# Two-layer graph network on one core: the order of squares, weights and stores between the layers, of the loads in the second layer, and of its last groups

## The chip, the core and the metric

The kernel runs on one core of one Trainium2 chip. The metric is the device time of one execution in microseconds (us), the median of three runs. A core has engines with a program each: PE (TensorE, matrix products; PEld is its loading of weights), DVE (VectorE), ACT (ScalarE), POOL (GpSimd) and SP (SyncE, which here only issues transfers). They meet at semaphores alone. DMA engines move the data between HBM and the on-chip memory; a transfer is issued by SP, by ACT or, for the indexed ones, by POOL.

## The reference

12,500 nodes with 16 features and 412,500 edges (200,000 random pairs both ways and one loop per node), sorted by the node `dst`.

```python
edge_index = jnp.stack([src, dst])
h = relu(layernorm(x));  x = x + L0(h, edge_index, edge_attr_16, ...)
h = relu(layernorm(x));  x = x + L1(h, edge_attr_8, ..., edge_index)

# L0: messages by a small network on the edge, summed, then normalized over the nodes
hid = relu(edge_attr @ W1 + b1); w = (hid @ W2 + b2).reshape(-1, 16, 16)
aggr = segment_sum(einsum('ei,eio->eo', x[src], w), dst)
out = aggr + x @ root + bias
out = relu((out - mean) / sqrt(var + 1e-5) * gamma + beta)      # over all nodes

# L1: a product of node and edge features, summed by node
m = silu(einsum('ei,ej,ijh->eh', x[dst], edge_attr, W_msg_tp) / sqrt(128)) @ W_msg_lin / 4
agg = segment_sum(m, src)
u = silu(einsum('ni,nh,ihk->nk', x, agg, W_upd_tp) / 16) @ W_upd_lin / 4;  return x + u
```

## The kernel before, in words

The program has five stages one after the other, with a barrier of all engines after each: `setup`, `layer0`, `between`, `layer1`, `finish`. The edges are cut into G = 404 groups of 1024 (T = 8 tiles of 128). The node arrays `k.agg`, `k.x`, `k.h` hold 128 nodes by 98 blocks (B = 98) of 16 features.

**between** (L1164). DVE, ACT and PE normalize the sums of layer 0 over the nodes: DVE subtracts the mean from `k.agg` in two halves (49 blocks each, L1249) and raises `bn_centred` after each; ACT squares each half into `sq` (L1307, `bn_squared`); DVE sums the squares (L1255); PE adds over the partitions (L1347); then come the root, the scaling, the new x, and the layer norm, again with squares by ACT (L1318), until DVE writes `k.h` in two halves (L1281), with `h1_ready` after each. Ahead of its squares ACT stands waiting for eight small loads of the message weights (`bd_in`) and copies them into another order (L1302, `bd_turned`); after its root it does the same for the update weights (L1311, `bdu_turned`). Then `NodeLinear` (`lin`, L640) computes Q = h @ W_msg_tp for all nodes: per chunk c of T = 8 blocks PE transposes h (`turn`, L660), ACT copies the transpose (L686), PE multiplies it by the weights in pieces of 4 blocks (L672). Q is kept as three bf16 parts: ACT or DVE makes the first (L1334, L1291), DVE the rest (L1296), ACT the second (L1324, `q_mid`), POOL the third (L1199, `q_lo`), 25 pieces in all. SP stores 8 blocks (two pieces) at a time to `q_rows` in HBM (L1222), 13 stores for the QB = 100 blocks.

**layer1** (L1354). Every engine walks over the groups with a body of its own; buffers are double (s = g % 2), and a ring of four holds what is scattered.
- SP, `load(g)` (L1421): waits until the group before last has used all buffers (`mult1`, `hotT_ready`, `same_ready`, `gathered`), reads the window of the group from `win_i` into a register, and issues four loads: `q_win` (the 128 rows of Q around the group's nodes), `ea` (the edges' 8 features), `dst_row` (the group's 1024 indices, broadcast to 128 partitions, L1417), `src_row` (512 indices, broadcast, L1439). For group 0 alone `dst_row` goes first. After group 3 SP loads `k.xp`; after the last group it stores `k.h` and loads it in another layout.
- DVE, `body(g)`: `unit(g,0)` (product of the gathered Q and `ea`, L1501), `residue(g-1)`, sum (L1510), `one_hot(g+1)` (L1483, from `dst_row`), `rows_to(g-2)` (L1557, the rows of the scatter), `unit(g,1)`, `low(g-1)`, `half_low(g-1)`, sum, `place(g-1)` (L1544), `columns(g-1)` (L1534), `same_source(g+1)` (L1490, from `src_row`).
- ACT, `body(g)`: silu and the high parts, `squares(g)` (L1643), `mid(g)`, `total_out(g-1)` and `rows_out(g-1)` (L1630, L1635), `columns(g)` (L1649).
- PE, `body(g)`: `gather(g)` (L1682, 24 products), `sum_wide(g-2)` (L1708, 32 products), `sum_rows(g-1)` (L1695, 12 products): 68 products a group.
- POOL: four indexed transfers per group which add `total` to the tables `sums` in HBM (L1745).

After the loop stand the last steps in order. DVE: `residue(G-1)`, `low`, `half_low`, `place`, `columns` of G-1, then `rows_to(G-2)`, `rows_to(G-1)`, the wait for all wide sums and the addition to `acc` (L1597). PE: `sum_rows(G-1)`, `sum_wide(G-2)`, `sum_wide(G-1)`, then 14 transposes of `acc` (L1733), which ACT copies (L1669) and SP stores (L1460, L1463). `sum_rows(g)` waits for `total_ready` of the group before. `place(g)` waits for the wide sum of g-2.

## Time and profile before

| what | value |
|---|---|
| time before, median of 3 runs | 7299.28 us (7299.2 to 7299.56) |
| the profiled execution, its span | 8221.3 us |
| PE, DVE, POOL, ACT busy | 89%, 81%, 69%, 54% of the span |
| layer 0, from the start's end to | about 4985 us |
| between | about 4985.6 to 5055.1 us |
| layer 1 | 5055.1 to about 8137 us |
| finish | to 8221.3 us |

The profiled execution has no time of its own beside its span, 8221.3 us; it is 922 us longer than the median of the runs without the profiler. Stretches are given in us from the span's start. An engine's busy time is the sum over which one of its instructions was running; the clock is the one granted to TensorE, 1.0 being 2.4 GHz and 0.5 being 1.2 GHz. Idle time before an instruction is put down to the one that released it.

### The profile page before, as it was taken

How to read it: one execution, taken by the hardware profiler on the slowest of the kernel's cores; microseconds unless marked ns; L12 is line 12 of the kernel's file. 1: busy time of each engine (PE TensorE's matmuls, PEld its weight loads, DVE VectorE, ACT ScalarE, POOL GpSimd, SP SyncE). 2: the span in 40 equal slices, each digit the busy share in tenths (PEclk: the TensorE clock that was granted, in tenths of full speed). 3: DMA queues.
4: the chain of work that ended last, by engine and by line, in shares of the span. 5: the costliest groups of instructions: out<-in, count | busy, mean ns of one | idle time of the engine just before them, and what ended most of it. 6: DMA issues, size and time to landing. Idle time of an engine off the chain costs nothing. (4 is left out here: it accounts for less than half of the span.)

```text
span 8221.3 us, 191064 instructions
## 1 busy us (share of the span) xinstructions
PE 7349.2 (89%) x52997; PEld 6446.6 (78%) x52997; DVE 6691.0 (81%) x17449; ACT 4457.4 (54%) x8279; POOL 5696.0 (69%) x4866
## 2 busy tenths in 40 slices
PE   7888888888888888888888886999999999999998
PEld 5667676666676666666676765999999999999996
DVE  6777777777777777777777777999999999999997
ACT  3333333333333333333333335888888878778884
POOL 6666666666666666666666664888888888888886
PEclk8999999999999999999999998999999999999999
DMA  2000000000000000000000014444444455554443
GB/s 60 18 17 17 17 17 17 17 17 17 17 17 17 17 18 17 17 17 18 17 17 17 17 23 101 73 75 74 74 75 74 74 73 74 72 74 75 73 75 64
DMA packets 713464, 341.73 MB, mean 42 GB/s; under 512 B 422115, under 2 KB 656599, under 8 KB 713427
## 3 DMA queue, kind: packets, MB, share of 16 engines
q1 hardware_dynamic: 379313, 272.94, 13.1%
q0 software_dynamic: 332928, 64.86, 12.9%
q10 hardware_dynamic: 1186, 3.51, 0.1%
q8 instruction: 15, 0.25, 0.0%
q14 instruction: 22, 0.18, 0.0%
HBM read 307.85 MB, written 32.96 MB: 41 GB/s over the span
## 5 line engine op out<-in xcount | busy, mean ns | idle before, releaser
L802 POOL DMA_INDIRECT xg<-gather_rows,idx x3132 | 3041.9, 971 | 1882.4 <-issue 1848.5
L919 PE MATMUL ps_w<-W2s,hT 128*128 128x256 f32 x12928 | 3240.2, 408 | 37.1 <-issue 36.6
L919 PEld LDWEIGHTS ps_w<-W2s,hT 128*128 128x128 f32 x12928 | 2678.5, 207 | 581.6 <-issue 97.0
L1745 POOL DMA_INDIRECT sums<-total,row x1616 | 2551.0, 1579 | 529.1 <-issue 474.4
L1708 PE MATMUL ps_wide<-hot_col,placed 128*128 128x392 f32 x12928 | 2434.7, 345 | 4.8 <-DVE placed L1544 2.1
L1708 PEld LDWEIGHTS ps_wide<-hot_col,placed 128*128 128x128 f32 x12928 | 2313.6, 196 | 12.2 <-issue 6.9
L841 ACT ACTIVATE hT<-ps_h,b1c 128x512 f32<-128x512 f32 x1616 | 1022.8, 680 | 2302.1 <-PE ps_h L905 2090.8
L1002 DVE TENSOR_TENSOR prod<-ps_w,xg 128x512 f32<-128x512 f32 x1616 | 1098.1, 690 | 969.7 <-remote 599.7
L1544 DVE SCALAR_TENSOR_TENSOR placed<-ps_r,src_r,halves 128x512 fp32r<-128x512 f32 x1616 | 1097.5, 741 | 0.1
L1643 ACT ACTIVATE square<-iota_col,minus_col 128x784 bf16<-128x784 int16 x1212 | 1061.3, 938 | 66.6 <-issue 58.0
L1009 DVE TENSOR_REDUCE msg<-prod 128x32 f32<-128x512 f32 x1616 | 1058.9, 676 | 0.0
L1649 ACT ACTIVATE hot_col<-square,ones 128x2352 fp32r<-128x2352 bf16 x404 | 910.4, 2253 | 0.0
L933 PE MATMUL ps_a<-parts,hot 128*128 128x48 bf16 x6464 | 347.5, 184 | 549.8 <-issue 534.0
L1033 DVE TENSOR_SCALAR hot<-iota,rel_t 128x256 bf16<-128x256 bf16 x3232 | 729.1, 303 | 116.0 <-DVE ea_res L982 73.0
L933 PEld LDWEIGHTS ps_a<-parts,hot 128*128 128x128 bf16 x6464 | 249.8, 96 | 580.4 <-issue 566.4
L905 PE MATMUL ps_h<-eT,W1p 96*128 96x512 bf16 x1616 | 526.5, 401 | 147.5 <-issue 137.8
L1682 PE MATMUL ps_q<-q_win,hotT 128*128 128x128 bf16 x9696 | 609.6, 219 | 18.9 <-DVE hotT L1483 18.9
L1501 DVE TENSOR_TENSOR prod<-ps_q,e 128x512 f32<-128x512 f32 x808 | 552.3, 684 | 42.6 <-issue 40.4
L1682 PEld LDWEIGHTS ps_q<-q_win,hotT 128*128 128x128 bf16 x9696 | 548.1, 98 | 20.0 <-DVE hotT L1483 20.0
L1510 DVE TENSOR_REDUCE pre<-prod 128x64 f32<-128x512 f32 x808 | 548.3, 679 | 0.1
L851 ACT ACTIVATE parts<-msg_res 128x128 bf16<-128x128 f32 x404 | 124.9, 309 | 552.9 <-DVE msg_res L1021 322.9
L835 ACT ACTIVATE eT<-ps_e 96x1024 bf16<-96x1024 bf16 x404 | 409.1, 1013 | 1.9 <-PE ps_e L895 1.9
(229 smaller groups left out, 5425.0 us busy)
## 6 DMA issues: line engine op xcount, KB each, us to landing
dst_row<-dst_rows SPq DMA_DIRECT2D x404, 256.0 KB
src_row<-src_rows SPq DMA_DIRECT2D x404, 128.0 KB
xg<-gather_rows,idx POOLq DMA_INDIRECT x3132
q_win<-q_rows SPq DMA_DIRECT2D x404, 96.0 KB
ea<-in_edge_attr SPq DMA_DIRECT2D x404, 64.0 KB
sums<-total,row POOLq DMA_INDIRECT x1616
e<-in_edge_attr SPq DMA_DIRECT2D x404, 32.0 KB
q_rows<-Q SPq DMA_DIRECT2D x12, 768.0 KB, 5.4
```

Source lines behind the costliest of these rows:

```text
L802: pool.indirect_dma_start(xg[r][:, t, :], None, k.rows, bass.IndirectOffsetOnAxis(ap=idx[r][:, t:t + 1], axis=0)).then_inc(xg_in[r][t], 16)
L841: a.activation(hT[s][:, j, :], ps_h[j][:, :], ACT.Relu, bias=k.b1[:, j:j + 1]).then_inc(q["relued"], 1)
L919: last = pe.matmul(to, hT[half][:, j, col:col + P], k.W2[:, j, :], start=(j == 0), stop=(j == 1 and not with_b2))
L1002: v.tensor_tensor(prod[u % 2][:, :, :, :], ps_w[u][:, :, :, :], xg[r][:, 2 * u:2 * u + 2, 0:D].unsqueeze(2).broadcast_to([P, 2, D, D]), AL ...
L1009: v.tensor_reduce(msg[s][:, 2 * u:2 * u + 2, :], prod[u % 2][:, :, :, :], X, ALU.add).then_inc(q["reduced0"], 1)
L1033: last = v.tensor_scalar(hot[s][:, t, :], k.iota[:, :], k.rel[:, bass.ds(g, 1), t:t + 1].rearrange("p g t -> p (g t)"), None, ALU.is_equal)
L1544: last = v.scalar_tensor_tensor(placed[s][:, w, :, :, :].rearrange("p r f a -> p r (f a)"), ps_r[:, :, :], src_r[:, bass.ds(g, 1), w], hal ...
L1643: last = a.activation(square[:, n, :], iota_col[:, :], ACT.Square, bias=minus_col[:, bass.ds(g, 1), WIDE - ACT_TILES + n])
L1649: a.activation(hot_col[s][:, WIDE - ACT_TILES:, :, :].rearrange("p w a b -> p (w a b)"), square[:, :, :].rearrange("p w b -> p (w b)"), AC ...
L1682: last = pe.matmul(ps_q[u][:, w, :, :].rearrange("p h j -> p (h j)"), hotT[s][:, t * P:(t + 1) * P], q_win[s][:, part * P:(part + 1) * P], ...
L1708: last = pe.matmul(ps_wide[:, 2 * r + a, 0:S.LC], placed[s][:, w, r * HR:(r + 1) * HR, :, part].rearrange("p r f -> p (r f)"), hot_col[s][ ...
L1745: pool.indirect_dma_start(k.sums[t], bass.IndirectOffsetOnAxis(ap=row[r][:, t:t + 1], axis=0), total[r][:, t, :], None, compute_op=ALU.add ...
```

## The change

Between the layers, ACT squares the halves before it waits for and copies the message weights; the products of h start when the first half of h is there, and the transpose of the chunk that reaches over the middle (c = 6) waits for the second; the first store of 8 blocks becomes two of 4. In layer 1, `load(g)` no longer waits for all four buffers at its head: `dst_row` goes first behind the wait for `hotT_ready`, the window register and `q_win` behind `gathered`, `ea` behind `mult1`, `src_row` behind `same_ready`. Behind the loop, DVE does `rows_to(G-2)` right after `residue(G-1)`, and PE `sum_wide(G-2)` before `sum_rows(G-1)`.

```diff
     def tensor(self, pe, ident, second_half=None):
         def turn(c):
+            if second_half is not None and (c + 1) * T > self.S.B // 2 >= c * T:
+                pe.wait_ge(second_half, 2)
             need(pe, self.copied, c - 1)
...
+    stores = [0, 4, *range(T, S.QB, T), S.QB]
...
-        for b0 in range(0, S.QB, T):
-            b1 = min(b0 + T, S.QB)
+        for b0, b1 in zip(stores, stores[1:]):
             sp.wait_ge(n["q_lo"], b1 // 4)
...
-        sp.wait_ge(n["q_stored"], 16 * S.NC)
+        sp.wait_ge(n["q_stored"], 16 * (len(stores) - 1))
...
+        for i, (b0, b1) in enumerate(HALVES):
+            a.wait_ge(n["bn_centred"], i + 1)
+            a.activation(sq[:, b0:b1, :], k.agg[:, b0:b1, :], ACT.Square).then_inc(n["bn_squared"], 1)
         a.wait_ge(n["bd_in"], 16 * T)
         a.activation(bd_msg[:, :, :].rearrange("p b (h j) -> p b h j", j=J),
                      bd_jh[:, :, :].rearrange("p b (j h) -> p b h j", j=J),
                      ACT.Copy).then_inc(n["bd_turned"], 1)
-        for i, (b0, b1) in enumerate(HALVES):
-            a.wait_ge(n["bn_centred"], i + 1)
-            a.activation(sq[:, b0:b1, :], k.agg[:, b0:b1, :], ACT.Square).then_inc(n["bn_squared"], 1)
...
-        pe.wait_ge(n["h1_ready"], 2)
-        lin.tensor(pe, k.ident[:, :])
+        pe.wait_ge(n["h1_ready"], 1)
+        lin.tensor(pe, k.ident[:, :], second_half=n["h1_ready"])
...
-                    need(sp, q["mult1"], (g - 1) * 2)
                     need(sp, q["hotT_ready"], g - 1)
-                    need(sp, q["same_ready"], g - 1)
+                    rows_of_dst(g, s)
                     need(sp, q["gathered"], (g - 1) * 2)
-                    first = isinstance(g, int) and g == 0
-                    if first:
-                        rows_of_dst(g, s)
                     at = sp.value_load(k.win_i[0:1, bass.ds(g, 1)], min_val=0, max_val=P * (S.QB - 1))
                     sp.dma_start(q_win[s][:, :], k.q_rows[bass.ds(at, P), :]
                                  ).then_inc(in_sems["win_in"][s], 16)
+                    need(sp, q["mult1"], (g - 1) * 2)
                     sp.dma_start(ea[s][:, :, :].rearrange("p t f -> p (t f)"),
...
-                    if not first:
-                        rows_of_dst(g, s)
+                    need(sp, q["same_ready"], g - 1)
                     sp.dma_start(src_row[s][:, 0:TP, :].rearrange("p t f -> p (t f)"),
...
                 residue(G - 1, 1)
+                rows_to(G - 2, 0)
                 low(G - 1, 1)
...
                 columns(G - 1, 1)
-                rows_to(G - 2, 0)
                 rows_to(G - 1, 1)
...
+                sum_wide(G - 2, 0)
                 sum_rows(G - 1, 1)
-                sum_wide(G - 2, 0)
                 sum_wide(G - 1, 1)
```

## Rows read from the trace of the kernel before

**Rows 1.** Busy time by stretch: layer 0. From-to, length, PE, PEld, DVE, ACT, POOL busy, clock, DMA, GB/s.
```profile
200.00:5000.00 4800.00, 4070.98 (x24518) 3322.83 (x24516) 3495.35 (x9684) 1876.42 (x3931) 2957.03 (x3049) 0.92 0.10 18
```

**Rows 2.** The same view, three stretches of layer 1.
```profile
5200.00:6570.00 1370.00, 1370.00 (x12408) 1339.22 (x12407) 1337.07 (x3282) 1108.13 (x1825) 1147.52 (x730) 1.00 0.49 74
6570.00:7360.00 790.00, 786.17 (x7058) 763.20 (x7055) 761.71 (x1871) 627.17 (x1037) 663.43 (x416) 1.00 0.56 73
7360.00:8080.00 720.00, 720.00 (x6526) 703.85 (x6525) 704.42 (x1728) 582.77 (x961) 602.93 (x385) 1.00 0.48 74
```

**Rows 3.** Groups by line, DVE, 6570 to 7360: busy us, mean ns, idle before.
```profile
L1483 DVE TENSOR_SCALAR hotT<-dst_row,node_id 128x1024 bf16<-128x1024 int16 x104 | 53.7, 516 | 19.7 <-DMA dst_row<-dst_rows 17.5 <-issue 1.1
```

**Rows 4.** Timeline of one ordinary group of layer 1: start, length, engine, line.
```profile
6506.33 0.68 DVE L1501 TENSOR_TENSOR prod<-ps_q,e 128x512 f32<-128x512 f32 x1
...
6508.90 0.33 SPq L1417 DMA_DIRECT2D dst_row<-dst_rows  x1
...
6510.96 0.74 DVE L1490 TENSOR_SCALAR same<-src_row,src_t 128x128 bf16<-128x128 int16 x4
...
6512.94 0.48 DVE L1483 TENSOR_SCALAR hotT<-dst_row,node_id 128x1024 bf16<-128x1024 int16 x1
```

**Rows 5.** Timeline, a group in the second stretch of rows 2.
```profile
7011.26 1.91 POOL L1745 DMA_INDIRECT sums<-total,row  x1 [0.30 <-issue]
7011.66 1.01 DVE L1490 TENSOR_SCALAR same<-src_row,src_t 128x128 bf16<-128x128 int16 x4
```

**Rows 6.** Timeline of the stage between the layers.
```profile
4991.50 1.95 ACT L1302 ACTIVATE bd_msg<-bd_jh 128x1024 f32<-128x1024 f32 x1 [11.02 <-DMA bd_jh<-in_L_gnn_W_msg_tp]
...
4993.36 1.59 ACT L1307 ACTIVATE bn_sq<-aggn 128x784 f32<-128x784 f32 x2
...
4994.23 2.84 DVE L1255 TENSOR_REDUCE bn_s<-bn_sq 128x16 f32<-128x784 f32 x2 [1.54 <-ACT bn_sq L1307]
...
5002.49 3.75 ACT L1311 ACTIVATE dst_t<-rel_t 128x2048 f32<-128x2048 f32 x1 [3.87 <-DMA rel_t<-in_L_gnn_W_upd_tp]
...
5007.81 1.74 ACT L1318 ACTIVATE bn_sq<-hn 128x784 f32<-128x784 f32 x2 [1.57 <-DVE hn L1270]
...
5012.08 1.86 DVE L1281 SCALAR_TENSOR_TENSOR hn<-hn,ln_sd 128x784 f32<-128x784 f32 x2
...
5019.31 27.93 POOL L1199 TENSOR_TENSOR Q<-q_res,Q 128x512 bf16<-128x512 f32 x25 [28.45 <-ACT Q L1324]
```

**Rows 7.** Stretches while Q is stored: from-to, length, clock, DMA share, GB/s.
```profile
5034.00:5038.00 4.00, 1.00 1.02 314
...
5053.00:5054.00 1.00, 0.50 0.54 170
```

**Rows 8.** Timeline of the first groups of layer 1.
```profile
5059.77 0.33 SPq L1417 DMA_DIRECT2D dst_row<-dst_rows  x1
...
5063.55 0.49 DVE L1483 TENSOR_SCALAR hotT<-dst_row,node_id 128x1024 bf16<-128x1024 int16 x1 [1.42 <-DMA dst_row<-dst_rows]
...
5071.16 0.49 DVE L1483 TENSOR_SCALAR hotT<-dst_row,node_id 128x1024 bf16<-128x1024 int16 x1 [3.17 <-DMA dst_row<-dst_rows]
```

**Rows 9.** Timeline of the last groups of layer 1.
```profile
8098.41 6.01 PE L1708 MATMUL ps_wide<-hot_col,placed 128*128 128x392 f32 x32
...
8110.43 0.62 DVE L1534 TENSOR_SCALAR hot_col<-iota_col,src_col 128x784 fp32r<-128x784 int16 x1
...
8111.58 0.47 PE L1695 MATMUL ps_sums<-parts,same 128*128 128x17 bf16 x12 [6.85 <-ACT total L1630]
...
8125.76 1.55 POOL L1745 DMA_INDIRECT sums<-total,row  x1 [0.30 <-issue]
8125.85 1.79 DVE L1597 TENSOR_TENSOR acc_wide<-acc_wide,ps_wide 128x1568 f32<-128x1568 f32 x1 [13.46 <-PE ps_wide L1708]
```

**Rows 10.** Stretches of 1 us at the end of layer 1: POOL busy, clock, DMA, GB/s.
```profile
8128.00:8129.00 1.00, 0.00 (x0) 1.00 0.32 7
...
8133.00:8134.00 1.00, 0.00 (x0) 0.85 0.67 233
```

More of the change, by code:

```diff
@@ L655, in bank, with tensor @@
         return self.out[s * self.pieces + j if self.pieces <= 2 else j]
-    def tensor(self, pe, ident):
+    def tensor(self, pe, ident, second_half=None):
         def turn(c):
+            if second_half is not None and (c + 1) * T > self.S.B // 2 >= c * T:
+                pe.wait_ge(second_half, 2)
             need(pe, self.copied, c - 1)
```

## Prediction

> **What bounds the kernel now.** I began with the busy time by stretch. The change touches nothing of layer 0, where PE is busy for 4071 of 4800 us [rows 1]; whatever makes the profiled execution 922 us longer than the median of the runs, most of it must lie there, because layer 1 has hardly an idle microsecond on PE to stretch: 1370.00 of 1370, 786.17 of 790, 720.00 of 720 us [rows 2]. So I take the savings found in the trace over to the median of 7299.28 us without scaling them, and widen the range for it.
>
> A group of layer 1 has 68 products on PE. 12408 of them in 1370 us are 182.5 groups of 7.51 us; 6526 in 720 us are 96.0 groups of 7.50 us. The reader is to see that these two stretches are PE's own time, with DVE close behind: 1337 / 182.5 = 7.33 us a group. The middle stretch differs. 7058 products are 103.8 groups in 790 us, 7.61 us each, at the same clock, and DVE's busy time per group is 7.34 us as before. What is new there is idle time of DVE, 17.5 us before `one_hot` until `dst_row` had landed [rows 3]; the DMA share is 0.56 instead of 0.49 for the same GB/s. The loads land later in this stretch, and DVE has only 7.51 - 7.33 = 0.18 us a group to absorb it.
>
> Then the timelines. In an ordinary group `unit(g,1)` ends at 6507.01, SP issues `dst_row` at 6508.90, behind the register load, `q_win` and `ea`, and `one_hot` reads it at 6512.94 [rows 4], 4.04 us after the issue. At the start of the layer a load took 5063.55 - 5059.77 = 3.78 us from issue to its reader [rows 8], so the ordinary margin is about a quarter of a microsecond.
>
> **The parts and their cost.**
>
> *Squares first.* DVE sat 1.54 us before the first sum of squares until ACT had them; ACT had been copying weights, 4991.50 to 4993.45 [rows 6]. Without that copy ahead ACT can square the first half as soon as it is centred: DVE's second pass and the masking end at 4994.23 - 1.54 = 4992.69, and one square (0.8 us) fits under them. The chain moves up by 1.5 us. The copy (1.95 us) now follows the squares and would end near 4995.6, while ACT's next work, the root, comes near 4997. If that cover were gone it would cost up to 1.95 us. Next in danger is the copy of the update weights, which doesn't move because its loads don't: it ends at 5006.24, and the squares of the layer norm, at 5007.81 now, want to start at 5006.3. They just fit, so 1.5 us survive.
>
> *Products from the first part.* PE starts after the first half of 1.86 us for two, 0.93 us sooner [rows 6]. Behind it DVE does the second half and the windows while PE and ACT turn the first chunks; the added wait stands at chunk 6, more than 10 us later, and costs nothing. If the half were late, PE alone would stand, and POOL behind it. Gain 0.9 us.
>
> *Two stores for one.* From the first piece on POOL is busy without a gap, 27.93 us for 25, 1.12 each [rows 6], but it is not the end: while Q is stored the DMA engines are full at 314 GB/s and go on until about 5053.5 [rows 7], 6.3 us after POOL. A store of 8 blocks is 786 KB, 2.5 us at that rate; POOL delivers one every 2.23 us. The first 4 blocks go out one piece (1.12 us) sooner, but the two half stores are drained at about P + 1.16 + 2.50 = P + 3.66 us (P is POOL's start) while the third is ready only at P + 4.51. Before, the first store was drained at P + 2.30 + 2.50 = P + 4.80. So the queue is ahead by 4.80 - 4.51 = 0.3 us and not by 1.12. Bounds 0 and 1.1; the extra issue on SP is hidden in its waits. Sum of this stage: 1.5 + 0.9 + 0.3 = 2.7 us.
>
> *Loads, at the start of the layer.* `dst_row` of group 1 stood behind the register load, `q_win` and `ea` at 5059.77; now it follows the loads of group 0, near 5057.9. The 1.42 us wait goes. That of group 2 was gated by the unit of group 0; now `one_hot(0)` and the place in SP's order gate it, near 5060.3, and with 3.8 us to land it is there at 5064.1, before DVE wants it (5071.16 - 3.17 - 1.42 = 5066.6). The 3.17 us wait goes too [rows 8]. The low parts, the placing and PE's first wide sum come behind these steps on DVE, so they move up by the sum, 4.6 us. Next in line is ACT's `mid(0)`, which moves with the units. Bounds 1.4 (only the first converts) and 4.9.
>
> *Loads, in the loop.* Every instruction of SP counts here: `load(g)` still ends behind the wait for `unit(g-2,1)`, with `ea` and `src_row`; but right behind these `dst_row(g+1)` follows, whose own gate, `one_hot(g-1)`, is already past (it stands before `unit` in DVE's body). It is issued about 1.2 us after the unit, some 7 us sooner than now for the group that needs it, and has near 11 us to land instead of 4.04 [rows 4]. `q_win` waits for PE's gather of the group before, which ends before that group's unit on DVE, so it too goes sooner than now. Nothing queued behind SP's new waits comes later than before. What the stretches say it is worth: 103.8 x (7.61 - 7.51) = 10.4 us, all in the middle one [rows 2]. In the other 280 groups PE has no idle time, and earlier loads bring nothing. Bounds: 0, if these late landings belong to the profiled execution alone or PE stays at 7.61 by another hand, and 11. I take 10.2, as the rows show DVE idle for 17.5 us there, more than the loss.
>
> *Last groups.* PE stood 6.85 us before `sum_rows(G-1)`, because ACT's total of G-2 came behind DVE's `rows_to(G-2)`, which stood behind `columns(G-1)`, ending 8111.05 [rows 9]. Now `rows_to(G-2)` (0.21 us) stands behind `residue`; its semaphore comes from PE's `sum_rows(G-2)`, finished just before, so what is queued behind (low, half_low, place) waits for nothing new. PE runs `sum_wide(G-2)` from 8104.7 to 8110.7 (6.0 us), `sum_rows(G-1)`, then from 8111.2 `sum_wide(G-1)` to 8117.2, against 8125.85 now: 8.7 us [rows 9]. What is late next is POOL, whose last transfer is issued at 8125.76 and moves bytes until near 8129, while the last store of the tables ends near 8133.7 [rows 9, 10]. POOL works without a gap in these groups and gains nothing from earlier rows. So the end of the layer moves from 8133.7 to POOL's, 8129 at best; how long POOL takes to close behind its last transfer the trace doesn't show. Bounds: 0.6 (POOL was almost the last already) and 8.7 (it isn't in the way when no profiler runs). I take 3.9, nearest to the row at 8129.
>
> The sum: 2.7 + 4.6 + 10.2 + 3.9 = 21.4 us. 8221.3 becomes 8199.9 in the profiled execution, 7299.3 becomes **7278**.
>
> **Where a rule speaks against it.** In the middle stretch one of POOL's four transfers per group took 1.91 instead of 1.55 us while DVE's four comparisons beside it took 1.01 us [rows 5] instead of 0.74 [rows 4]. The Trainium skill, SBUF — State Buffer, "Who interferes with whom", says that DVE in its two-port modes and GpSimd share one pair of ports under an exclusive lock, and whoever comes second blocks; by that rule every group could fall into this state, and the sum would be the 7332 us of the last rival below.
>
> **The rivals.** *The loop gives nothing.* The late landings are the profiled execution's, or DVE's waits are covered by PE. For it: 300 of 404 groups have no such wait. Against: the time per group rises exactly where DVE waits. Gain 2.7 + 4.6 + 3.9 = 11.2, time 7288. Chance 0.22.
>
> *The loads don't come sooner.* SP is in order; if `dst_row(g+1)` were held by what stands ahead of it (`src_row(g)` behind its gates), the 4.04 us stay. Against: that gate is the unit of g-2, a group earlier. Gain 2.7 + 3.9, at the start perhaps 1.4: 7291. Chance 0.04.
>
> *Slower: DVE and POOL meet at a worse phase.* The place is DVE's `same_source` beside POOL's transfer. The price is 1.01 - 0.74 = 0.27 us a group on DVE. It decides once it exceeds DVE's spare 0.18 us: 7.34 + 0.27 = 7.61 against 7.50, times 404, is 44 us, less the 11 of the other parts: 7332. For it: POOL is issuing all the time and the phase is set by who waits for what. Against: in the two long undisturbed stretches the phase holds by itself, and the change removes what disturbed it. Chance 0.07.
>
> **How the numbers follow.** A measurement of this kernel can tell about 0.2%, 14.6 us, from no change. The forecast and its neighbours hold 0.67; they lie below 7284.7 unless the loop gives under a third of its 10. The two small cases (0.26) are within 0.2%, the phase case is slower (0.07). For the range, downwards the tail can bring 4.8 and the stores 0.8 more, with the start's 0.3 down to 7272, and some for the unscaled carry-over; upwards it takes in 7288 and 7291. So 7267 to 7292.
>
> **What would show it.** In the profile after: no idle time before DVE's first sum of squares; POOL's first piece about 2.4 us earlier against the stage's start; `dst_row` waits gone from DVE, at the start and in the stretch near 6570 to 7360; 7.50 us a group throughout; PE's 6.85 us gone from the tail and POOL's last transfer ahead of the barrier. I am wrong if the middle stretch keeps 7.6 us without `dst_row` waits, if POOL's transfers of 1.91 us spread over all groups, or if the barrier after layer 1 follows 8125 rather than 8129.

## The result and the profile after

The changed kernel takes 7283.83 us (median of 17 runs, 7281.98 to 7288.34), the kernel before 7299.20 us (17 runs beside them, 7295.09 to 7305.03). The ratio is 0.9981, with a 95% interval of 0.9975 to 0.9987: 15.4 us, or 0.21%, less. The forecast was 7278 us, 21.4 us less, within 7267 to 7292. The direction and the range held; the gain is about three quarters of what was forecast.

One thing must be known to read the profiles. The rows ahead of the prediction come from an execution of 8221.3 us. The profiled execution of the changed kernel has a span of 7286.6 us and a time of 7288.34 us, the longest of the 17 by only 0.6 us. So the profiler is not what cost 922 us. The second set of experiments ran on a chip on which the kernel before takes 8229.26 us (21 runs, 8227.04 to 8233.75), and there too unprofiled executions are as long as profiled ones (one kernel: 8199.57 us with the profiler, 8194.03 to 8198.97 in four runs without). The rows ahead come from an execution of that kind, the median forecast for from the other. Below they are "the 8229-us chip" and "the 7298-us chips". Medians are compared only within one chip, and stages within one kind of chip; where a profile after stands beside the rows ahead, which are of the other kind, `c_before` is given too. A profile of the kernel before on a 7298-us chip came with the first experiments (`c_before`).

The table (us) is worked out from the starts of instructions in the timelines. *Between* runs from POOL's memset that opens the stage to the first issue of `dst_row`. *Start* runs from there to PE's row sums of group 1, *loop* to those of group G-2 (401 groups), and *tail* to the first load of `finish`. `c_after` and `c_after2` are further profiles of the changed kernel.

| kernel | span | setup and layer 0 | between | start | loop | tail |
|---|---|---|---|---|---|---|
| before, the rows ahead (8229-us kind) | 8221.3 | 4985.6 | 69.5 | 27.1 | 3022.0 | 33.0 |
| `c_before` (7298 us) | 7304.5 | 4083.1 | 70.0 | 28.9 | 3005.4 | 32.8 |
| after | 7286.6 | 4079.5 | 67.1 | 24.1 | 3003.5 | 27.5 |
| `c_after` | 7286.2 | 4080.7 | 67.8 | 22.2 | 3003.5 | 27.6 |
| `c_after2` | 7286.6 | 4079.7 | 67.5 | 24.3 | 3003.5 | 27.0 |

From `c_before` to the mean of the three profiles of the changed kernel: between 2.5, start 5.3, loop 1.9, tail 5.4, in all 15.1 us, against 15.4 in the median. Setup and layer 0 differ by another 3.2 us; the kernels of the first set, none of which touches them, lie between 4080.7 and 4083.6 there, so this is spread.

**The loop.** Busy time by stretch of the changed kernel, columns as in rows 1; it answers to [rows 2] and, for layer 0, to [rows 1]:

```profile
200.00:4000.00 3800.00, 3653.18 (x24002) 2933.17 (x24000) 3361.41 (x9445) 1842.75 (x3855) 2861.57 (x2989) 1.00 0.11 21
4300.00:7100.00 2800.00, 2800.00 (x25415) 2738.06 (x25414) 2749.31 (x6728) 2246.34 (x3740) 2344.29 (x1496) 1.00 0.48 74
```

PE has no idle time in 2800 us, and the loop takes 3003.48 / 401 = 7.490 us a group; no group is over 7.55. Layer 0 has a clock of 1.00 here and 0.92 in [rows 1]. Groups by line over that stretch, DVE, which answers to [rows 3] (busy us, mean ns, idle before):

```profile
L1481 DVE TENSOR_SCALAR hotT<-dst_row,node_id 128x1024 bf16<-128x1024 int16 x374 | 178.0, 476 | 0.0
```

No wait is left. The timeline of an ordinary group, with DVE's next comparison, which answers to [rows 4]:

```profile
5701.33 0.33 SPq L1430 DMA_DIRECT2D q_win<-q_rows  x1
...
5702.74 0.33 SPq L1433 DMA_DIRECT2D e<-in_edge_attr  x1
5703.17 0.38 SPq L1437 DMA_DIRECT2D src_row<-src_rows  x1
...
5704.10 0.34 SPq L1419 DMA_DIRECT2D dst_row<-dst_rows  x1
...
5709.20 0.48 DVE L1481 TENSOR_SCALAR hotT<-dst_row,node_id 128x1024 bf16<-128x1024 int16 x1
...
5716.35 0.47 DVE L1481 TENSOR_SCALAR hotT<-dst_row,node_id 128x1024 bf16<-128x1024 int16 x1
```

SP's order is as forecast: `ea` after the unit, `src_row`, then `dst_row` of the next group 1.4 us after `ea`. By the order of the code the comparison at 5709.20 reads an earlier issue; that of 5704.10 is read one group later, at 5716.35. So the margin, the time from the issue to its reader, is 12.3 us (forecast: near 11) where it was 4.04.

**Between.** Timeline, columns as in rows 6; the stage starts at 4079.52 here and started at 4985.59 in [rows 6]:

```profile
4085.29 0.86 ACT L1305 ACTIVATE bn_sq<-aggn 128x784 f32<-128x784 f32 x1 [10.88 <-DVEq L1254]
4086.68 0.86 ACT L1305 ACTIVATE bn_sq<-aggn 128x784 f32<-128x784 f32 x1 [0.53 <-DVEq L1254]
4086.74 2.86 DVE L1257 TENSOR_REDUCE bn_s<-bn_sq 128x16 f32<-128x784 f32 x2
4087.45 1.92 ACT L1307 ACTIVATE bd_msg<-bd_jh 128x1024 f32<-128x1024 f32 x1
...
4100.34 1.74 ACT L1320 ACTIVATE bn_sq<-hn 128x784 f32<-128x784 f32 x2 [0.20 <-DVE hn L1272]
...
4105.73 0.66 PE L662 MATMUL msg_pt<-ident,hn 128*128 128x128 f32 x2 [15.03 <-DVE hn L1283]
...
4111.12 8.97 POOL L1202 TENSOR_TENSOR Q<-q_res,Q 128x512 bf16<-128x512 f32 x8 [26.34 <-ACT Q L1326]
```

The squares stand ahead of the weights' copy, and DVE's sum of squares has no idle time before it. From the stage's start the first sum comes at 7.2 us instead of 8.6, the squares of the layer norm at 20.8 instead of 22.2, POOL's first piece at 31.6 instead of 33.7. Forecast were 1.5 and, together, 2.4 us. The copies of the weights are hidden, as supposed. The stage as a whole went from 69.5 to 67.1 us: 2.1 us at POOL's first piece, and 0.3 behind it for the stores. This sets profiles of two kinds of chip side by side. In `c_before` POOL's first piece comes at 34.3 us, and in the three profiles of the changed kernel at 31.6, 32.1 and 32.0, so within one kind it is 2.4 us by their mean, and some 0.2 for the stores.

**Start of layer 1.** Timeline, which answers to [rows 8]:

```profile
4146.65 0.35 SPq L1419 DMA_DIRECT2D dst_row<-dst_rows  x1
...
4149.89 0.49 DVE L1481 TENSOR_SCALAR hotT<-dst_row,node_id 128x1024 bf16<-128x1024 int16 x1 [2.75 <-DMA dst_row<-dst_rows]
...
4153.33 0.48 DVE L1481 TENSOR_SCALAR hotT<-dst_row,node_id 128x1024 bf16<-128x1024 int16 x1
...
4157.67 0.47 DVE L1481 TENSOR_SCALAR hotT<-dst_row,node_id 128x1024 bf16<-128x1024 int16 x1
...
4162.88 8.02 PE L1706 MATMUL ps_wide<-hot_col,placed 128*128 128x392 f32 x32 [1.86 <-DVE hot_col L1532]
```

Both waits (1.42 and 3.17 us) are gone; only group 0 waits for its first load. PE's first wide sum starts 16.23 us after the layer's start, against 21.26 in the execution of [rows 8] and 21.21 in `c_before`: 5.0 us sooner. But it takes 8.02 us instead of the 6.02 it took in the execution of [rows 8]. The busy time by stretch shows why (columns as in rows 1, PE alone):

```profile
4158.00:4160.00 2.00, 0.97 (x24) 1.00 0.59 176
4160.00:4162.00 2.00, 1.02 (x16) 0.63 0.83 80
4162.00:4164.00 2.00, 1.12 (x4) 0.50 0.97 276
4164.00:4166.00 2.00, 2.00 (x8) 0.50 0.96 206
```

The clock was at 2.4 GHz (1.00), PE was busy for 0.97 of 2 us, and in the next stretch the clock fell to 1.2 (0.50); two of the five microseconds went back. In `c_after` PE was busy for 0.99 and 0.82 us of the two stretches ahead of that sum and the clock stayed at 1.00; the sum took 6.02 us, and the start is 22.2 us instead of 24.1. Nor is the slow sum a thing of the change. In `c_before` the clock stood at 0.50 until about 4178, some way into its first wide sum:

```profile
4174.37 7.83 PE L1708 MATMUL ps_wide<-hot_col,placed 128*128 128x392 f32 x32 [0.82 <-DVE placed L1544]
```

**Last groups.** Timeline, which answers to [rows 9]:

```profile
7180.41 0.47 PE L1693 MATMUL ps_sums<-parts,same 128*128 128x17 bf16 x12
7181.11 6.02 PE L1706 MATMUL ps_wide<-hot_col,placed 128*128 128x392 f32 x32 [0.24 <-issue]
7187.17 1.79 DVE L1595 TENSOR_TENSOR acc_wide<-acc_wide,ps_wide 128x1568 f32<-128x1568 f32 x1 [6.03 <-PE ps_wide L1706]
...
7191.89 0.39 SPq L1458 DMA_DIRECT2D sums<-rel_t  x1
...
7195.47 1.55 POOL L1743 DMA_INDIRECT sums<-total,row  x1 [0.30 <-issue]
...
7201.71 0.32 SPq L1818 DMA_DIRECT2D acc<-sums  x1
```

PE's 6.85 us are gone, and DVE's addition comes 12.96 us after the row sums of G-2 instead of 21.59, 8.6 us sooner (forecast 8.7; in `c_before` it was 21.41). The stage ends only 5.4 us sooner: POOL's last transfer starts at 7195.47, 3.6 us behind the first store of the tables, and `finish` begins 4.7 us after the 7197.02 at which it ends. By this POOL is the last now; the last experiment tests it.

### The profile page after: what moved, and what is told of

It reads as the page before. It is cut to its first block and busy times, and to the rows that moved or that the text cites. A ratio compares the mean times of both kernels' runs of the same rounds, so it can differ in the third digit from the quotient of the medians.

```text
span 7286.6 us, 190461 instructions
## 1 busy us (share of the span) xinstructions
PE 6987.3 (96%) x52997; PEld 6106.2 (84%) x52997; DVE 6660.5 (91%) x17449; ACT 4439.4 (61%) x8279; POOL 5640.9 (77%) x4866
## 5 line engine op out<-in xcount | busy, mean ns | idle before, releaser
L804 POOL DMA_INDIRECT xg<-gather_rows,idx x3132 | 3003.5, 959 | 1008.4 <-issue 971.7
L921 PE MATMUL ps_w<-W2s,hT 128*128 128x256 f32 x12928 | 2958.9, 382 | 48.3 <-DVE prod L1004 47.0
L921 PEld LDWEIGHTS ps_w<-W2s,hT 128*128 128x128 f32 x12928 | 2433.8, 190 | 538.4 <-DVE prod L1004 158.7
L1004 DVE TENSOR_TENSOR prod<-ps_w,xg 128x512 f32<-128x512 f32 x1616 | 1079.4, 689 | 232.3 <-issue 59.5
L849 ACT ACTIVATE parts<-msg 128x128 bf16<-128x128 f32 x404 | 125.0, 309 | 876.6 <-DVE msg L1017 876.6
L1680 PE MATMUL ps_q<-q_win,hotT 128*128 128x128 bf16 x9696 | 607.3, 219 | 18.0 <-DVE hotT L1481 16.2
L907 PE MATMUL ps_h<-eT,W1p 96*128 96x512 bf16 x1616 | 483.2, 380 | 7.4 <-ACT hT L843 6.3
L897 PEld LDWEIGHTS ps_e<-identb,ea_parts 128*96 128x96 bf16 x3232 | 202.8, 123 | 177.8 <-DVE ea_parts L991 165.3
```

What stands on the lines that cost most here:

```text
L804: pool.indirect_dma_start(xg[r][:, t, :], None, k.rows, bass.IndirectOffsetOnAxis(ap=idx[r][:, t:t + 1], axis=0)).then_inc(xg_in[r][t], 16)
L921: last = pe.matmul(to, hT[half][:, j, col:col + P], k.W2[:, j, :], start=(j == 0), stop=(j == 1 and not with_b2))
L1004: v.tensor_tensor(prod[u % 2][:, :, :, :], ps_w[u][:, :, :, :], xg[r][:, 2 * u:2 * u + 2, 0:D].unsqueeze(2).broadcast_to([P, 2, D, D]), AL ...
L1680: last = pe.matmul(ps_q[u][:, w, :, :].rearrange("p h j -> p (h j)"), hotT[s][:, t * P:(t + 1) * P], q_win[s][:, part * P:(part + 1) * P], ...
```

## The experiments

The expectations speak of theories A and B on the loop. By A the late landings belong to every execution of the kernel before, and the new order of the loads saves some 10 us there. By B they belong to the execution of the rows ahead, and the gain lies in the start, the tail and between. The intervals of single parts reach about 0.09% either way, 6 to 7 us, so a part is read from the stages of its profile and the median only has to agree.

### The two kernels again, with profiles on the same chip

No edit. The kernel before:

> The kernel before, once more, for an ordinary profile of it. Theory A (the loop's gain is real in every execution): its profile again has a stretch of layer 1 with dst_row waits and 7.6 us a group, and layer 1 lasts about 3082 us as in the first profile. Theory B (that stretch was an accident of the first profiled execution): no such stretch, about 7.51 us a group throughout, layer 1 about 3072 us, and dst_row waits on DVE only at the layer's start (4.6 us in two waits). Time against itself: ratio 1.000.

The kernel after:

> The changed kernel, once more beside the others. Both theories: 0.998 of before; between the layers 67.1 us, layer 1 about 3055 us, 7.49 us a group, first wide sum of layer 1 at 1.2 GHz again if the clock falls at the same place.

`c_before` took 7297.44 us (11 runs; ratio to 33 runs of the same kernel 0.9999, 0.9990 to 1.0008), `c_after` 7285.13 us (0.9981, 0.9972 to 0.9990). The loop of `c_before` is 3005.36 us, 1.9 more than the changed kernel's 3003.48, and only 6 of 401 groups are over 7.55 us, against 69 in the rows ahead. Yet the cause is there in small. Busy time of the stretch with the waits, DVE's group row over 4300 to 7100, and two waits of that stretch, of ACT and of DVE (us in all, times, longest):

```profile
5650.00:6440.00 790.00, 789.03 (x7177) 770.96 (x7176) 773.13 (x1895) 632.39 (x1052) 661.67 (x420) 1.00 0.55 74
```
```profile
L1483 DVE TENSOR_SCALAR hotT<-dst_row,node_id 128x1024 bf16<-128x1024 int16 x373 | 180.1, 483 | 10.3 <-DMA dst_row<-dst_rows 9.5
```
```profile
ACT total L1630 <- DMA sums<-total,row: 55.6, 63, 1.8
...
DVE hotT L1483 <- DMA dst_row<-dst_rows: 9.1, 21, 0.9
```

The DMA share is 0.55, as in the middle line of [rows 2], and DVE waits 9.1 us, half of the 17.5 of [rows 3]; but PE is idle for 0.97 us, not 3.83. Waits of 0.4 us on DVE are mostly made good before PE needs the result. So on this chip B is nearly right for the loop. The two runs also settle the start: it was 28.9 us, not 27.1, and of the changed kernel's three profiles one has the fast first wide sum.

### The loads alone

```diff
# on the kernel before
-                    need(sp, q["mult1"], (g - 1) * 2)
                     need(sp, q["hotT_ready"], g - 1)
-                    need(sp, q["same_ready"], g - 1)
+                    rows_of_dst(g, s)
                     need(sp, q["gathered"], (g - 1) * 2)
-                    first = isinstance(g, int) and g == 0
-                    if first:
-                        rows_of_dst(g, s)
...
+                    need(sp, q["mult1"], (g - 1) * 2)
...
-                    if not first:
-                        rows_of_dst(g, s)
+                    need(sp, q["same_ready"], g - 1)
```

> The kernel before with only the change of the loads in layer 1. Theory A: start 3 to 4.6 us and loop 10 us less, ratio 0.998 (-14 us). Theory B: start 3 us (the first wide sum runs at 1.2 GHz and gives 2 back) and, going by 7.49 instead of 7.51 us a group, up to 7 us in the loop: -3 to -10 us, ratio 0.9986 to 0.9996. Stage between the layers 69.5 us as before.

7292.41 us (11 runs), ratio 0.9992 (0.9983 to 1.0001). Start 24.2 (28.9 in `c_before`), loop 3003.48, tail 33.6, between 69.8: the loads give 4.7 at the start and 1.9 in the loop, 6.6 us, against 6.1 in the median. The tail, which the edit doesn't touch, is 0.7 us longer than in `c_before`: so much differs between profiles.

### The order of the last groups alone

```diff
# on the kernel before
                 residue(G - 1, 1)
+                rows_to(G - 2, 0)
...
-                rows_to(G - 2, 0)
...
+                sum_wide(G - 2, 0)
                 sum_rows(G - 1, 1)
-                sum_wide(G - 2, 0)
```

> The kernel before with only the new order of the last groups. From PE's last row sums inside the loop (group G-2) to the first load of the last stage: 33.0 us before, 27.5 with the whole change. If POOL's last transfer is what ends the layer now, it is 27.5 here too and POOL's last transfer ends 4.7 us ahead of the stage's end; PE's wide sums end 8.7 us sooner. Time -4 to -5.5 us, ratio 0.9993 to 0.9995 (theories A and B alike). If half the gain needs the earlier loads, it is over 29 us.

7293.39 us (11 runs), ratio 0.9994 (0.9985 to 1.0003). Tail 27.65 instead of 32.83, 5.2 us; the median is 5.1 less. Start (28.6) and between (69.9) are as before. The loop, with the loads as before, took 3004.40 us here, 0.9 us above the 3003.5 of every kernel with the new loads on these chips, where `c_before` is 1.9 above it; so the loop's gain is 1 to 2 us. The two parts and between's share of about 2.2 add up to 13.4, and `c_after` is 13.4 below its runs of before: nothing is lost or doubled between the parts.

### Between alone, and the change without the loads

These two, and the next two, ran on the 8229-us chip. The first has the hunks of the diff on `tensor`, the stores, ACT's squares and PE's wait alone; the second has the whole change, with `load(g)` as before:

```diff
# the change without the loads, on the changed kernel
+                    need(sp, q["mult1"], (g - 1) * 2)
                     need(sp, q["hotT_ready"], g - 1)
-                    rows_of_dst(g, s)
+                    need(sp, q["same_ready"], g - 1)
                     need(sp, q["gathered"], (g - 1) * 2)
+                    first = isinstance(g, int) and g == 0
+                    if first:
+                        rows_of_dst(g, s)
...
-                    need(sp, q["mult1"], (g - 1) * 2)
...
                                  ).then_inc(in_sems["e8_in"][s], 16)
-                    need(sp, q["same_ready"], g - 1)
+                    if not first:
+                        rows_of_dst(g, s)
```

> The kernel before with only the three edits between the layers (squares first, products from the first half, first store in two). The stage lasts 67.1 us instead of 69.5, and layer 1 starts as before, with dst_row waits of 1.4 and 3.2 us on DVE. Time -2.4 us, ratio 0.9997: at the edge of what can be told.

> The changed kernel with the loads of layer 1 as before. Theory A (loads are worth 14 us): 1.0 to 1.2 us per thousand only remain, ratio 0.9990 (-7 us). Theory B (loads are worth 3 to 10): the same -7 us, since this kernel has all of the change but them; what differs is the gap to the changed kernel, 14 us or 3 to 10. Its loop at 7.51 us a group if the loads set it, 7.49 if they do not.

Between alone: 8228.43 us (11 runs), ratio 1.0000 (0.9991 to 1.0009); its stage is 67.6 instead of 69.5, 1.9 us, which the interval of the whole can't show. Without the loads: 8223.91 us, 0.9993 (0.9984 to 1.0002); between 67.3 and tail 28.0, 2.2 and 5.0 us less than in the rows ahead, sum 7.2, median 5.4. Both keep the long loop, 3023.7 and 3022.6 us, with 81 and 85 groups over 7.55.

### All pieces of Q stored one by one

The whole change, and 25 stores of 4 blocks instead of two of 4 and then 8 at a time. It was made to see whether the DMA engines still stand idle while Q is stored; on this chip it is also the kernel with the new loads.

```diff
-    stores = [0, 4, *range(T, S.QB, T), S.QB]
+    stores = [*range(0, S.QB + 1, 4)]
```

> The changed kernel with all 25 pieces of Q stored one at a time. In the changed kernel the DMA share falls to 0.75 and 0.42 for two us after the two half stores, 0.8 us lost. If the queue is short of data there, this closes the gap and the stage lasts 66.2 to 66.4 us instead of 67.1. If each transfer has a cost of its own on the engines, 25 stores are longer than 14 and it is above 67.1. In the total not measurable (0.8 us).

8197.62 us (5 runs), ratio 0.9959 (0.9945 to 0.9972). Two things came out. **The stores.** Stretches while Q is stored (from-to, length, clock, DMA share, GB/s), the changed kernel:

```profile
4114.00:4115.00 1.00, 1.00 1.02 316
4115.00:4116.00 1.00, 1.00 0.75 239
4116.00:4117.00 1.00, 1.00 0.42 134
4117.00:4118.00 1.00, 1.00 1.03 325
```

and about the same time from the stage's start in this kernel:

```profile
5025.00:5026.00 1.00, 1.00 0.81 263
5026.00:5027.00 1.00, 1.00 1.02 319
5027.00:5028.00 1.00, 1.00 1.00 310
5028.00:5029.00 1.00, 1.00 1.04 320
```

The changed kernel's DMA engines are idle for 0.25 + 0.58 = 0.83 us after its second store, as the prediction's count said (they are drained at P + 3.66 and the third comes at P + 4.51, 0.85 us). One by one the gap is closed and the stage takes 66.5 us, 0.6 to 1.3 less than in the three profiles of the changed kernel. In the whole time that can't be told.

**The loads on this chip.** From the kernel without them, the median is 26.3 us less: start 27.2 to 22.7, loop 3022.6 to 3004.3, and 0.9 us in between and the tail. By stage that is 23.7 us. The two kernels differ in the 25 stores too, which end before layer 1; the changed kernel itself didn't run on this chip. Here A holds, and more than A: 18.4 us in the loop. In the kernel without them the time above 7.490 us a group was 12.3 us between groups 200 and 312 and 6.9 us in all the others. Busy time by stretch, 6570 to 7360, without and with the new loads:

```profile
6570.00:7360.00 790.00, 786.86 (x7066) 763.43 (x7064) 763.96 (x1871) 628.56 (x1040) 653.86 (x416) 1.00 0.56 73
```
```profile
6570.00:7360.00 790.00, 790.00 (x7188) 772.42 (x7187) 773.80 (x1899) 636.36 (x1056) 661.32 (x423) 1.00 0.46 75
```

The DMA share falls from 0.56 to 0.46 while the bytes rise from 73 to 75 GB/s, and PE gets through 122 products (1.8 groups, 13 us) more. The waits of the same stretch, without (engine and line, waited for: us, times, longest):

```profile
ACT total L1632 <- DMA sums<-total,row: 102.3, 89, 2.0
...
DVE hotT L1485 <- DMA dst_row<-dst_rows: 7.6, 18, 0.8
```

and with the new loads:

```profile
ACT total L1628 <- DVE row_f L1555: 88.2, 105, 1.0
ACT square L1641 <- PE ps_wide L1706: 59.0, 104, 0.7
```

DVE's waits alone, 7.6 us, are less than the 13 us lost. The other wait that goes here is ACT's before it writes `total`, for the indexed transfers that still read the old one: 102.3 us in 89 groups, up to 2.0 at once. The prediction didn't look at it. But its sum says little of a loss. On a 7298-us chip the same wait stays with the new loads, with no group over 7.55 us (`c_after`, 5650 to 6440):

```profile
ACT total L1628 <- DMA sums<-total,row: 38.7, 53, 0.7
```

There `c_before` had 55.6 us in 63 groups, up to 1.8. What the new loads shorten on both kinds is the longest of these waits, so the indexed transfers do end less late; that this carried part of the 18.4 us is argued and not shown, and how much of the loss ran over ACT and how much over DVE wasn't separated.

### Idle TensorE filled with products

This adds products of the identity matrix that nobody reads, so the clock should be up at the first gather and the first wide sum. It was made because the start is partly run at 1.2 GHz.

```diff
# on the kernel with the 25 stores; 80 such products end the stage between
+                def warm(n):
+                    for _ in range(n):
+                        pe.matmul(ps_wide[:, 0, 0:P], k.identb[:, :], k.identb[:, :], ...)
                 def body(g, s, use):
+                    if isinstance(g, int) and g < 3:
+                        warm((30, 0, 24)[g])
                     gather(g, s, use)
+                    if isinstance(g, int) and g == 2:
+                        warm(16)
```

> As the one before, with products of the identity on PE, into memory that nobody reads, where it idles at the end of the stage between the layers and in groups 0 to 2 of layer 1. If the first wide sum is 2 us long because PE had idled and its clock had fallen to 1.2 GHz, the clock stays at 2.4 GHz, the first wide sum takes 6.0 instead of 8.0 us, the first gathers 1.5 instead of 2.7, and from the start of layer 1 to the row sums of group 1 it is 24.1 - 2 to 3 = 21 to 22 us. If the clock falls nevertheless, 24.1 or more. Time -2 to -3 us against the one before.

8197.70 us (5 runs), ratio 0.9961 (0.9947 to 0.9974): no change against the kernel without them. Timeline:

```profile
5056.85 3.36 PE L1721 MATMUL ps_wide<-identb 128*128 128x128 bf16 x30 [9.75 <-PEq L106]
...
5061.04 2.72 PE L1684 MATMUL ps_q<-q_win,hotT 128*128 128x128 bf16 x24 [0.84 <-DMA q_win<-q_rows]
...
5070.40 2.72 PE L1721 MATMUL ps_wide<-identb 128*128 128x128 bf16 x24
```

PE stood for 9.75 us at the barrier ahead of them, the clock was at 0.50 and stayed there; the first gather took 2.72 us (1.50 at full clock), and the products themselves pushed later work back: the start is 25.2 us, against 22.7. The expectation, 2 to 3 us less, was missed. The first wide sum took 6.03 us, but without the products, in the kernel with the 25 stores, it took 6.02 as well. So that profile had no slow wide sum to mend, and the experiment shows only what the products cost; whether they keep the clock up where it would fall stays open.

### What in the load order matters

On a third chip (the kernel before: 7297.81 us, 25 runs) the changed kernel ran again, and beside it two that put all four waits back at the head of `load(g)`. In one, `dst_row` is issued first behind them:

```diff
# on the changed kernel
+                    need(sp, q["mult1"], (g - 1) * 2)
                     need(sp, q["hotT_ready"], g - 1)
-                    rows_of_dst(g, s)
+                    need(sp, q["same_ready"], g - 1)
                     need(sp, q["gathered"], (g - 1) * 2)
+                    rows_of_dst(g, s)
...
-                    need(sp, q["mult1"], (g - 1) * 2)
...
-                    need(sp, q["same_ready"], g - 1)
```

and in the other last (but for group 0), behind `src_row`, one issue later than in the kernel before:

```diff
# on the changed kernel, with the four waits at the head as above
...
                                  ).then_inc(in_sems["srow_in"][s], 16)
+                    if not first:
+                        rows_of_dst(g, s)
```

> The changed kernel beside the three below. 0.998 of before where before takes 7298 us, 0.996 (about 30 us less) where it takes 8229 us. Loop of layer 1 7.490 us a group.

> The changed kernel, but with all four waits at the head of the load as in the kernel before, and dst_row issued first behind them. It is issued 1.9 us sooner than in the kernel before, not 7. If dst_row's margin of 4.0 us is what costs, 5.9 us are enough: loop within 2 us of the changed kernel's 3003.5, no waits for dst_row in the middle groups; at the start of the layer it is 1 to 3 us slower than the changed kernel, since group 2's load is still gated by the unit of group 0. If it is the waits for the other buffers that matter, the loop is as in the kernel before, 3005 or 3022 us.

> The changed kernel with all four waits at the head and dst_row issued last, behind src_row: the margin falls from 4.04 to 3.6 us. With 3.4 to 3.8 us from issue to landing, DVE waits for it in most groups, 0 to 0.4 us; it can absorb 0.18. A loop of 7.5 to 7.7 us a group: 10 to 80 us more than the changed kernel, ratio to before above 1.000. If DVE's waits for dst_row are covered by PE even so, the ratio stays at 0.999.

The changed kernel: 7283.56 us (10 runs), 0.9981 (0.9971 to 0.9991). `dst_row` first: 7284.17 us (10 runs), 0.9980 (0.9971 to 0.9990), the same. `dst_row` last: 7380.44 us (4 runs), 1.0113 (1.0096 to 1.0130), 97 us more than the changed kernel; the expectation was 10 to 80. DVE's group rows over the whole span, of the first:

```profile
L1481 DVE TENSOR_SCALAR hotT<-dst_row,node_id 128x1024 bf16<-128x1024 int16 x404 | 193.1, 478 | 4.0 <-DMA dst_row<-dst_rows 4.0
```

and of the last, with the busy time of its stretch of late landings:

```profile
L1485 DVE TENSOR_SCALAR hotT<-dst_row,node_id 128x1024 bf16<-128x1024 int16 x404 | 205.9, 510 | 104.5 <-DMA dst_row<-dst_rows 103.8
```
```profile
5650.00:6440.00 790.00, 726.59 (x6447) 697.49 (x6445) 709.28 (x1700) 567.19 (x946) 587.96 (x380) 1.00 0.50 67
```

So the separate waits, which are most of the change's lines in `load`, are worth nothing measurable in the loop; `dst_row`'s place ahead of `q_win` and `ea` is what counts, though with the common head its margin, 6.45 us in one ordinary group (issued at 5704.29, read at 5710.74), is half that of the changed kernel. That in the late groups its transfers are then as short as elsewhere may have a part in it (see what stays open). At the start the separate waits bring about 1.2 us, too little for the whole time: the first wide sum begins 17.6 us after the layer's start in this kernel, against 16.2 to 16.5. And the kernel before stood at an edge. One more issue ahead of `dst_row`, some 0.4 us, makes DVE wait for it for 103.8 us in the whole layer and 94.0 in the loop (111 groups, up to 1.5 at once), the loop longer by 93.5 us (3096.96), and groups of 790 / (6447 / 68) = 8.33 us in the stretch, 108 in all over 7.55. There the waits come through to PE almost in full (94.0 to 93.5): in the stretch DVE waits 80.4 us for `dst_row`, and PE is idle 54.5 us until DVE's placing ends. In `c_before` 9.5 us of these waits in the loop (22 groups, up to 0.9) cost 1.9.

### POOL's last transfers left out

This leaves out the four indexed transfers of the last group, so the sums of its 1024 edges are missing from the tables.

```diff
# on the changed kernel
                 def scatter(g, r, lap):
+                    if isinstance(g, int) and g == G - 1:
+                        return
...
-                    pool.wait_ge(added[t], 16 * G)
+                    pool.wait_ge(added[t], 16 * (G - 1))
```

> The changed kernel without the four indexed transfers of the last group (their sums are left out of the tables). If POOL's last transfer ends layer 1 now, its tail, 27.6 us from the last row sums inside the loop, shortens until the chain of PE, the copies and the stores of the table ends it: first addition to acc at 13.0, plus 1.8, 2.9 and 3.5 us, plus 3 us of barrier, near 24.2; gain 3 to 3.5 us. If POOL is not the bound, the tail stays at 27.5.

7280.57 us (10 runs), ratio 0.9976 (0.9967 to 0.9986), 3.0 us less than the changed kernel. The tail is 24.4 instead of 27.0. Timeline:

```profile
7184.63 1.79 DVE L1595 TENSOR_TENSOR acc_wide<-acc_wide,ps_wide 128x1568 f32<-128x1568 f32 x1 [6.03 <-PE ps_wide L1706]
...
7189.34 0.39 SPq L1458 DMA_DIRECT2D sums<-rel_t  x1
...
7196.07 0.32 SPq L1820 DMA_DIRECT2D acc<-sums  x1
```

With POOL out of the way the stage closes 6.7 us behind the first of these stores, as it did in all four profiles with the old order of the last groups (6.71 to 6.73 us; in `c_before` from 7213.52 to 7220.23) and as SP's own chain would have it in the changed kernel: 7191.89 + 6.7 = 7198.6, and there the stage closed at 7201.7. So POOL bounds the tail in the changed kernel, and the chain over DVE, PE and SP's stores ends 3 us before it. In all nine profiles with the new order and all of POOL's transfers it closes 4.6 to 4.8 us behind the end of the last one. The four transfers add up to 7.4 us of POOL's work (1.85 us apart), of which 3.0 show in the time.

## Why the prediction was right, and where it wasn't

**Squares first, 1.5 us, and the first part of h, 0.9.** POOL's first piece is 2.4 us sooner than in `c_before` by the mean of three profiles, and 2.4 were forecast; on the 8229-us chip, with these edits alone, it is 1.6 sooner than in the rows ahead. The squares brought 1.4. The wait at chunk 6 cost nothing. The copy of the update weights stayed hidden. **Two stores for one, 0.3.** The whole stage gained 2.5 us, of 2.7 forecast, and the DMA gap that the count foresaw, 0.85 us, was measured at 0.83 us and closed by the experiment with 25 stores. On the 8229-us chip the stage gained 1.9 and 2.2 us.

**The start of the layer, 4.6 us.** Measured 5.3 by the mean of three profiles, 4.7 by the loads alone. Both waits went, and the first wide sum came 4.9 us sooner than in `c_before` by the mean of the three. In two of three profiles that sum then ran partly at the lower clock and took 2 us more, a thing the prediction didn't consider. The stage still gained 5.3 because the same happened in `c_before`, where that sum took 7.83 us and the start 28.9 us; in the rows ahead it took 6.02, and the start 27.1. Of the 5.3 us, 4.9 are the earlier start of that sum and 0.5 its mean length, which is the clock's and differs from one execution to the next.

**The loop, 10.2 us: the step that failed.** "103.8 x (7.61 - 7.51) = 10.4 us, all in the middle one" was read from an execution of the 8229-us kind and taken over to a median of the other kind. The cause was right on both: late landings, most of them in the same stretch of groups, gone with the new order. The term is 1 to 2 us on the chips of the median (1.9 from `c_before`). On the 8229-us chip it is 18.4, because the other stretches, at 7.50 and 7.51 us a group, also had something to lose (7.490 after), which the prediction had put at nothing; whether ACT's wait for the indexed transfers counted beside DVE's wasn't shown. The prediction explained the 922 us as lying in layer 0, which the table bears out: 4985.6 against about 4080 us for setup and layer 0. Its error was to conclude that layer 1 would be alike but for that. A trace whose span is 12.6% off its median is of another execution in every stage until shown otherwise. The rival of 11.2 us, where the loop gives nothing, is 4.2 us off the measured 15.4, the forecast 6.0; on the median's chips the loop was nearer to that rival.

**The last groups, 3.9 us.** Measured 5.4 (5.2 alone). The order on DVE and PE gained 8.6 us as forecast (8.7), and POOL took the rest, as forecast. What was under-sized is where POOL lets go: 3.9 rested on a row at 8129, "at best"; the layer now ends 4.7 us after POOL's last transfer, and in the rows ahead that interval behind 8125.76 + 1.55 would have ended near 8132.0, while the stage closed near 8137.3. The end of DMA work near 8133.7 and the row at 8129 were both taken for ends of the stage, 3.6 and 3.0 us too early, which hid 0.6 us of the gain; another 0.8 is the prediction's own step from 8133.7 - 8129 = 4.7 down to 3.9, for which it had no row.

**The sum.** 2.7 + 4.6 + 10.2 + 3.9 = 21.4 forecast; 2.5 + 5.3 + 1.9 + 5.4 = 15.1 by stage, 15.4 in the median. Without the loop's 8.3 us too many the forecast would have been 2 us too small. That the measured time lies inside the range owes to the range having been drawn wide enough to take in the case in which the loop gives nothing.

**The rivals.** That the loads don't come sooner fell: the margin is 12.3 us. The worse phase of DVE and POOL didn't appear: of POOL's 1616 indexed transfers of layer 1, 57 took over 1.7 us in `c_before` and 8 in the profile after, and there no group is over 7.55 us. The rule of the Trainium skill, SBUF — State Buffer, "Who interferes with whom", was weighed against the sum; single transfers of POOL still take longer than 1.55 us here (one of 2.01 in the tail), but nothing of it reaches PE's 7.490 us a group, so the blocking that the rule speaks of, if it is what lengthens them, cost no time in this kernel.

**What stays open.** Why setup and layer 0 take some 900 us more on one chip than on the others. The clock there, 0.92 in place of 1.00, is the smaller part: from 200 to 4000 us PE is busy for 166 ns per product in the execution of the rows and for 152 in `c_before`, but idle for 29 against 6. The costliest instructions of DVE and ACT there are as fast in both (690 and 689 ns, 680 and 680); the waits between them are longer. Why the late landings sit in the same groups, some 204 to 311, on both kinds of chip: in the packed trace a transfer of `dst_row` (first to last packet, median) lasts 2.8 to 3.0 us there, and 1.8 to 2.1 elsewhere; its last packet is 3.8 to 3.9 us behind the issue in these groups of the kernel before, against the margin of 4.04, and 2.9 to 3.1 us elsewhere. With the new order it lasts 1.9 us in these groups too. They vanish when `dst_row` and `src_row` of the same group are not read one behind the other, but that this is the cause is argued and not shown. Why the clock is down for the first wide sum in one execution and not in the next.

## What to carry to other kernels

For each load in a loop compare the time from its issue to its reader with the time that it takes to land; where the two are close (here 4.04 us against 3.78, or 3.8 to 3.9 to the last packet in the late groups), put that load first in the queue, because one more issue ahead of it can cost far more (97 us here) than moving it gains. Check that the profiled execution is of the kind whose median you forecast before you carry a stage's saving over, stage by stage. Behind a shortened tail, look for the engine that closes last: here 8.6 us off DVE and PE were worth 5.4, for POOL.

## What the hardware showed that wasn't expected

- The same kernel takes 7298 us on two chips and 8229 us on a third, with all runs of it within 0.15% of each other on each. The difference lies in setup and layer 0 (about 4083 against 4986 us), and some 17 us of it in the second layer's loop.
- A margin acts like a cliff: in the loop, waits for `dst_row` of 9.5 us in all (up to 0.9) cost 1.9 us in the kernel before on a 7298-us chip, and 94.0 us (up to 1.5) cost 93.5 with the issue one place later. In the rows' execution 17.8 us of them stood beside a loop 18.5 us too long.
- Late landings go together: with `dst_row` late, ACT waited up to 2.0 us at once for POOL's indexed transfers (102.3 us in the stretch from 6570 to 7360 on the 8229-us chip), and with the new order of the loads there was no such wait in that stretch, although the bytes per second rose from 73 to 75 GB/s while the DMA share fell from 0.56 to 0.46. On a 7298-us chip the longest fell from 1.8 to 0.7 us, and 38.7 us of such waits in 790 cost nothing.
- TensorE's clock went from 2.4 back to 1.2 GHz where PE had been busy for 0.97 of 2 us, and the next wide sum took 8.02 us in place of 6.02; in another execution of the same kernel, with PE busy for 0.82 of 2 us, it stayed up. Some 3.4 us of small products behind 9.75 us of idleness didn't raise it.
- From the end of POOL's last indexed transfer to the next stage's first load 4.6 to 4.8 us pass, in all nine profiles in which POOL ends last; without the four last ones the stage ends 3.0 us sooner, and the stores of the tables are then the last.
